# Giving GpSimd the last 395 of 1601 columns of a subtraction that DVE did alone

## The reference

```python
x = x + xattn(layernorm(x), ctx, mask, ...)   # 1601 keys a batch, one head, width 128
x = x + ffn(layernorm(x), ...)                # rms norm, 8 experts, top 2, gated (silu), 128 -> 2*256 -> 128
# in xattn
Q = h @ Wq + bq;  K = ctx @ Wk + bk;  V = ctx @ Wv + bv
scores = where(mask == 0, -1e9, Q @ K.T / sqrt(128));  out = softmax(scores) @ V
```

## Time and profile before

| what | value |
|---|---|
| median of 3 runs | 450.25 us (450.22 to 450.42) |
| the profiled execution | 450.19 us, of which the span of instructions is 448.3 us |
| TensorE busy | 396.9 us, 89% of the span |
| weight loads busy | 361.5 us, 81% |
| DVE busy | 345.0 us, 77% |
| ScalarE busy | 267.5 us, 60% |
| GpSimd busy | 252.8 us, 56% |
| data moved | 68.66 MB, mean 153 GB/s |

### The profile page before, as it was taken

One profiled execution on the slowest core, in us unless ns is written; L12 is line 12 of the kernel. 1 busy time (PEld: TensorE's weight loads), 2 busy tenths in 40 slices (PEclk: granted clock), 3 DMA queues, 4 the chain that ended last, 5 costly groups with the idle time before them and its releaser, 6 DMA issues. The chain is left out here.

```text
span 448.3 us, 10369 instructions
## 1 busy us (share of the span) xinstructions
PE 396.9 (89%) x2742; PEld 361.5 (81%) x2742; DVE 345.0 (77%) x1453; ACT 267.5 (60%) x642; POOL 252.8 (56%) x347
## 2 busy tenths in 40 slices
PE   2598999999999999999999999777989999999960
PEld 1598999999999999999999989756878788888750
DVE  2486888898898898898898898655776676777772
ACT  1165666656656656656656645424757677777750
POOL 1063244566566566566566574436777766566670
PEclk9989999999999999999999999776999999999995
DMA  4954473483483483483483350231223643338526
GB/s 125 326 150 171 166 264 95 162 281 97 171 280 105 165 283 104 164 283 107 159 284 111 154 168 21 59 86 30 74 84 102 158 117 87 84 90 285 193 67 217
DMA packets 60824, 68.66 MB, mean 153 GB/s; under 512 B 6096, under 2 KB 52320, under 8 KB 60768
## 3 DMA queue, kind: packets, MB, share of 16 engines
q1 hardware_dynamic: 56192, 58.52, 40.7%
q0 software_dynamic: 4544, 9.38, 6.3%
q10 hardware_dynamic: 32, 0.10, 0.1%
HBM read 54.41 MB, written 13.57 MB: 152 GB/s over the span
## 5 line engine op out<-in xcount | busy, mean ns | idle before, releaser
L1280 PE MATMUL ps<-attention,ctx_sb 128*128 128x128 f32 (+1 forms) x832 | 116.4, 282 | 10.5 <-ACT attention L704 4.8
L1280 PEld LDWEIGHTS ps<-attention,ctx_sb 128*128 128x128 f32 (+1 forms) x832 | 103.6, 195 | 17.7 <-issue 11.2
L631 POOL DMA_INDIRECT parts<-mbias,blk_x x78 | 77.8, 997 | 39.7 <-ACT mbias L771 31.5
L704 ACT ACTIVATE attention<-ps 128x512 f32<-128x512 f32 x96 | 56.5, 597 | 36.4 <-PE ps L1262 32.4
L537 POOL TENSOR_TENSOR rstd<-ve,minus_half 128x2 f32<-128x2 f32 x32 | 26.8, 837 | 90.0 <-DVE ve L894 90.0
L574 POOL DMA_INDIRECT rows_in<-kept,place x64 | 67.5, 1054 | 13.2 <-issue 12.7
L1262 PE MATMUL ps<-ident,attention 128*128 128x128 f32 (+1 forms) x416 | 68.4, 281 | 0.0
L838 DVE CUSTOM_DVE_ANT_0 attention<-ps,mbias 128x1608 f32<-128x1608 f32 x32 | 58.6, 1830 | 4.3 <-issue 4.3
L678 ACT ACTIVATE attention<-attention,ebias 128x1601 f32<-128x1601 f32 x32 | 52.0, 1624 | 10.9 <-DVE ebias L856 10.7
L1185 DVE SCALAR_TENSOR_TENSOR ctx_sb<-ctx_sb,ps 128x256 f32<-128x256 f32 x78 | 32.8, 420 | 33.0 <-ACT ctx_sb L758 32.2
L1246 PE MATMUL ps<-ctxt_high,gt_high 128*128 128x402 f32 x128 | 48.3, 378 | 5.0 <-DVE ctxt_low L980 3.0
(11 more groups left out here) (132 smaller groups left out, 828.4 us busy)
## 6 DMA issues: line engine op xcount, KB each, us to landing
ctxt_in<-ctx_cols SPq DMA_DIRECT2D x16, 800.5 KB
mbias<-mbias_dram SPq DMA_DIRECT2D x16, 800.5 KB, 5.7
ctx_sb<-ctx_rows SPq DMA_DIRECT2D x16, 768.0 KB
blk_x<-rows_in SPq DMA_DIRECT2D x78, 65.0 KB, 1.9
attention<-parts SPq DMA_DIRECT2D x8, 512.0 KB, 5.2
x_in<-x SPq DMA_DIRECT2D x16, 128.0 KB, 4.7
wup_in<-w_up_t SPq DMA_DIRECT2D x8, 256.0 KB, 5.1
out<-base_all SPq DMA_DIRECT2D x8, 256.0 KB, 3.1
```

Of the source, the lines that this page charges most:

```text
L631: pool.indirect_dma_start(parts, bass.IndirectOffsetOnAxis(ap=blk_x[:, m % XR, D:D + 1].bitcast(I32), axis=0), blk_y[:, m % YR], None).the ...
L704: act.activation(probs_t[:, g * BANK:(g + 1) * BANK], ps_turn[:, g % 2], ACT.Copy).then_inc(s_pt_act, 1)
L1280: last = pe.matmul(ps_o[:, 0:P], ctx_sb[0:n, j, t], probs_t[0:n, t * P:(t + 1) * P], start=t == 0, stop=t == KT - 1)
```

## The change

After the change DVE subtracts the first SHARE = 3 x 402 = 1206 columns, and GpSimd, in a new function `split_rest`, the last 395. GpSimd's part has a semaphore of its own, `s_ctxt_rest`. SyncE's load of `ctxt_in` and each of TensorE's scores wait for both semaphores. On GpSimd the subtraction is the first thing of the even slots u = 0 to 28; that of batch 0 stands between the two first reciprocal roots, ahead of the tables.

```diff
--- before.py
+++ after.py
@@ -88,6 +88,7 @@
     CH = 4
     assert E == PAIRS and GU[0] % 4 == 0 and GU[1] % 4 == 0 and GU[0] <= ROOM and GU[1] <= ROOM
 
+    SHARE = 3 * CW
     LATE_SLOTS = [1, 4, 7]
     LAST_RANK = 10
     FILL_LOAD = 28
@@ -256,6 +257,7 @@
         s_ctxt = sem("ctxt_loaded")
         s_ctxt_high = sem("ctxt_high")
         s_ctxt_low = sem("ctxt_low")
+        s_ctxt_rest = sem("ctxt_low_rest")
         s_mask = sem("mask_loaded")
         s_mrows = sem("mask_bias_made")
         s_mstore = sem("mask_bias_stored")
@@ -382,6 +384,7 @@
                 sp.dma_start(x_in[:, j], x_tiles[b]).then_inc(s_x[j], 16)
 
                 wait(sp, s_ctxt_low, b)
+                wait(sp, s_ctxt_rest, b)
                 sp.dma_start(ctxt_in[:], ctx_cols[b]).then_inc(s_ctxt, 16)
                 if isinstance(i, int) and b == 0:
                     sp.wait_ge(s_mstore, 16)
@@ -513,8 +516,19 @@
                 wait(pool, s_xn1, 2 * i + j)
                 pool.tensor_tensor(rstd1[:], ve1[:], minus_half[:], ALU.pow).then_inc(s_rs1, 1)
 
+            def split_rest(b):
+
+                j = b % 2
+                pool.wait_ge(s_ctxt_high, b + 1)
+
+                wait(pool, s_scores, QT * (b - 1))
+                pool.tensor_tensor(ctxt_low[:, j, SHARE:SK], ctxt_in[:, SHARE:SK], ctxt_high[:, j, SHARE:SK].bitcast(F32),
+                                   ALU.subtract).then_inc(s_ctxt_rest, 1)
+
             def slot_first(i, k):
                 u = 4 * i + k
+                if k % 2 == 0 and is_unit(u + 2):
+                    split_rest(u // 2 + 1)
                 if is_unit(u - 2):
 
                     pool.wait_ge(s_y, u - 1)
@@ -585,6 +599,7 @@
                                pattern=[[-1, P]], channel_multiplier=1).then_inc(s_ident, 1)
             pool.tensor_copy(iota_f[:], iota_i[:]).then_inc(s_iota, 1)
             rstd_of_x(0, 0)
+            split_rest(0)
             rstd_of_x(0, 1)
 
 
@@ -977,7 +992,7 @@
                 dve.wait_ge(s_ctxt_high, b + 1)
 
                 wait(dve, s_scores, QT * (b - 1))
-                dve.tensor_tensor(ctxt_low[:, j, 0:SK], ctxt_in[:], ctxt_high[:, j, 0:SK].bitcast(F32),
+                dve.tensor_tensor(ctxt_low[:, j, 0:SHARE], ctxt_in[:, 0:SHARE], ctxt_high[:, j, 0:SHARE].bitcast(F32),
                                   ALU.subtract).then_inc(s_ctxt_low, 1)
 
             def split_up_weights(e):
@@ -1238,6 +1253,7 @@
                 j = k // 2
                 pe.wait_ge(s_gtc, 2 * i + j + 1)
                 pe.wait_ge(s_ctxt_low, 2 * i + j + 1)
+                pe.wait_ge(s_ctxt_rest, 2 * i + j + 1)
 
                 wait(pe, s_max, u)
                 for c in range(SCORE_CHUNKS):
```

## The result

The changed kernel takes 463.1 us (median of 4, 460.94 to 465.77), the kernel before beside it 450.34 (450.22 to 451.69): a ratio of 1.028, 95% interval 1.022 to 1.034. It is slower by 12.8 us, where 3 us faster was forecast.

What follows compares the result with a forecast made beforehand. TensorE was taken as the bound, with only holes in its stream to win: 11 x 0.29 = 3.2 us gained, 0.2 and 0.1 lost in early slots, -2.9 us from 450.25 to 447.3 us; range 445.5 to 450.6.

Steps and rivals of the forecast that it cites:

- The next bound, 0.29 us further on: Even slots: with the hole before L1223 gone, L1280 waits for ScalarE's L704, so 0.29 us is gained per slot.
- rival (a): DVE's whole 0.41 us counts in each of 11 slots, as L704 is not the next wait: 446.0 us; chance 0.13.
- SyncE's load: Next `ctxt_in` load, released 0.44 us later; over 1 us of slack estimated, cost nothing; without slack up to 4.8 us.
- The extra semaphore: One more wait before each of TensorE's 32 scores: taken as 0, bounded at 1 us in all.
- Rival (d): SyncE's load waits for both parts and has no slack, each batch from slot 8 0.44 us longer: 455.0 us; chance 0.05.
- Who comes first holds the other off: Settled even slots: DVE's subtraction begins first, so GpSimd's part starts after it and ends 0.85 us behind.
- The sign that the prediction had named for this: Forecast wrong if DVE's subtraction starts later than 1.1 us after GpSimd's reciprocal root L537 in settled slots.
- (c): GpSimd reaches its subtraction first in settled slots too, making DVE's 0.58 us later in each of 11: 457.2 us; chance 0.08.
- (e), the clock: TensorE's granted clock may shift in a stretch: about 1 us either way, in the range, no chance of its own.
- The early slots: GpSimd's subtraction may delay DVE's L908: slot 2 loses 0, slot 4 0.2, slot 6 0.1 us; bounds 0.5 gained, 1.8 lost.
- an iota lets L908 pass: Slot 6: DVE's second norm L908 gets through, but the cast L1129 is caught, 0.1 us lost.
- The third load: Slot 1: GpSimd's part of batch 1 gates the issue of the third `ctxt_in`; taken as 0, bounds 0.4 gained, 0.6 lost.

Runs made afterwards that it cites:

- 1: The kernel before with DVE's subtraction cut to 1206 columns, the last 395 left zero and nothing given to GpSimd: 446.51 us (ratio 0.992).
- 3: The changed kernel with GpSimd's part of the subtraction moved into the odd slot before, where GpSimd is idle: 446.87 us (ratio 0.996).
- 8: GpSimd's part in the odd slot before, as in 3, but DVE alone subtracts batches 0 and 1: 447.24 us (ratio 0.993).
- 17: The changed kernel with GpSimd's part also waiting for DVE's cast of the places, from the sixth slot on: 448.88 us (ratio 0.995).
- 18: As 12, with the residual base behind the scatter, but 128 columns for GpSimd instead of 395: 449.83 us (ratio 1.000).
- 12: The changed kernel with GpSimd's residual base moved behind the slot's first scatter, in even slots from 6 on: 461.55 us (ratio 1.025).
- Experiment 7: The changed kernel without DVE's cast of the places; the sum ahead of it is written as int32 at once: 461.22 us (ratio 1.023).
- experiment 10: The changed kernel with one of the two waits ahead of GpSimd's part, the one for the scores, removed: 461.22 us (ratio 1.025).
- 4: The changed kernel with GpSimd's part in its place, but first waiting for the norm's `y` as the residual base does: 459.71 us (ratio 1.021).
- 9: The kernel before with a second, already fulfilled wait ahead of GpSimd's residual base: 450.93 us (ratio 1.000).

## Why the prediction was wrong

**Right.** Which wait bounds the even slot and what DVE's part is worth in it: 1.40 us for the subtraction, 16.51 for the batch (16.5 forecast), 3.4 us for the whole (3.2). The next bound, 0.29 us further on, also fits: the period fell by 0.26 and not by 0.41, so rival (a) is out, and L1280 stood behind L704 (1). The cost of GpSimd's columns: 1.05 us (0.99). SyncE's load cost nothing in the change: ScalarE doesn't wait for `ctxt_in` after slot 1. The extra semaphore cost nothing (3 has it, at the period of 1), nor did DVE's L874 to L838 (L889 took 0.35). Where the hold is away and everything is computed, the time is 446.87 (3), 447.24 (8) and 448.88 (17), around the 447.3 forecast.

**In part luck.** The 3.4 us of experiment 1 are not 11 times 0.29. In its profile the subtraction of slot 6 starts 0.55 us earlier than before, which was forecast at nothing, and the eleven batches from there to slot 28 give 2.7, so 0.25 each. And the "over 1 us of slack" of SyncE's load was wrong, though it did no harm: in the kernel before ScalarE waits for `ctxt_in` at 167.6 and 200.8, for 0.56 and 0.21 us, and in 17, where GpSimd's part ends later, three times after slot 1, for up to 0.88, at a period of 16.53. Rival (d)'s wait exists, but it did not set the period.

**Wrong: one step**, "Who comes first holds the other off. [...] So GpSimd starts after DVE's shortened L980". Its evidence was L521, which gave way in this place. That row is of 128 columns. At 128 columns L525 gives way as well (18), at 395 it does not (12). The row answered for an instruction of its own size, and I carried it over to one three times as long. The sign that the prediction had named for this came: 1.1 us behind the end of the reciprocal root was the latest start for DVE's subtraction, and it starts 2.41 behind (150.73 against 148.32). So in place of 0.29 us gained in each slot there were 0.90 lost. GpSimd's part, forecast at 1.8 to 2.3 us with most of it waiting, took 1.05.

Two smaller mistakes go with it. The step looked at L980 alone, while the cast L1129 stands ahead of it and is caught first; I had the cast in view only for slot 6. And I set the start of GpSimd's row against the start of DVE's, 142.51 against 142.19, as if the rows showed the order of the claims. Experiment 7 has a claim about 0.6 us ahead of its recorded start, and in 17 L525 has the same recorded start, 0.49 us behind the cast's, and holds nothing.

**The rivals.** (c) had the right sign and about the right place, at a chance of 0.08 and with too small a price: 0.58 us a slot, where 0.90 were lost. And its condition, that scatter and iota take 0.32 us less, was not met: both are as before (1.10 and 0.16). Of the 0.32 us between the two prices 0.06 is GpSimd's longer part (1.05 for 0.99). That the rest is the claim ahead of the recorded start fits, but is argued. (e), the clock, was bounded at 1 us; in the profiled change the 1.2 GHz level lasted from before 38 to after 44, and it and the late load cost 3.5 us together.

**The early slots.** In slots 2 and 4 the second norm was held by L525 as forecast. In slot 6 "an iota lets L908 pass" was wrong: it was held there too, and the cast not. In experiment 10, whose slot 1 lost nothing, the copy of slot 5 comes 0.12 us later than before and the subtraction of slot 6 starts 0.93 later, so slot 6 cost 0.8 us where 0.1 was forecast. Slot 4 cost about the 0.2 forecast (the copy goes from 0.06 early in slot 2 to 0.11 late in slot 4).

```profile
44.76 1.04 DVE L923 TENSOR_SCALAR y<-x,mv,rstd 128x128 f32<-128x128 f32 x1
...
78.33 1.16 DVE L923 TENSOR_SCALAR y<-x,mv,rstd 128x128 f32<-128x128 f32 x1
80.03 0.17 DVE L1144 CAST place<-place_f 128x4 int32<-128x4 f32 x1
```

The third load was bounded at 0.6 us lost. At the copy of slot 1 the profiled execution of the change was 3.5 us behind, that of 4 was 1.0 behind (with the clock at 0.50 from 39 to 41) and that of 10 nothing. The reason given, a later issue, is not what happened: the issue was at 30.69, before at 30.72. What makes the load arrive late was not settled: with the first two batches all on DVE the wait is short and the spread narrow (8), but 18, which has GpSimd's part there, has a short wait too (1.53), and 9, which has none of it, a long one (2.95).

**Open.** Why 128 columns give way and 395 do not. The table fits a claim that is made for what is ready behind the scatter and given up when only about 0.5 us of it is left, but no run shows such a rule at work, and lengths between 128 and 395 were not tried. Nor was the number of columns told apart from the time that they take.

## What to carry to other kernels

Before an instruction is put on GpSimd beside DVE work, look for the DVE instructions that will come up while it is ready, not only while it is recorded as running, and take the evidence from a row of the same length. Where GpSimd has idle time in a stretch in which DVE reads PSUM or one tensor, put the work there (3), or make it wait for the DVE instruction that must go first (17). And a part of the gain that looks safe is best tried without the risky part: experiment 1 showed by itself that DVE's part gains and the loss had to come with what was added.

## What was not expected of the hardware

A DVE cast of 4 columns took 1.58 us, asked for 0.50 us ahead of the recorded start of the GpSimd instruction that held it. The Trainium skill ("SBUF — State Buffer", Who interferes with whom) says that whoever issues first gets the shared pair, and "Issue order, not op shape, decides who blocks." By the recorded starts this case speaks against both: the order was the same at 128 and at 395 columns, 0.49 to 0.50 us in DVE's favour, and the size decided. Experiment 17 agrees with the first sentence, if issue is when an instruction is ready and not when its row starts. But the 128 columns of 18 were ready as early as the 395 of 12 and gave way, so that reading doesn't cover the size either.

The same section lists `cast` and `tensor_scalar` among those that can contend, and lets a `tensor_reduce` on this chip never do so; by that the trace agrees: the cast and L923 were held, while in experiment 7 the `tensor_reduce` asked for 0.11 us ahead of the held subtraction took its 0.18. (No row shows that GpSimd's claim stood already when it began, so for `tensor_reduce` this is weak evidence.)
